# When a group's input rows are loaded in the query stage

## What is computed

```python
h = modulate(layernorm(x), shift_msa, scale_msa)
qkv = h @ W_qkv + b_qkv                  # 576 -> 3 * 576
o = softmax(q * scale @ k.T) @ v         # 16 heads of 36
x = x + gate_msa * (o @ W_proj + b_proj)
x = x + gate_mlp * (gelu(modulate(layernorm(x)) @ W_fc1 + b_fc1) @ W_fc2 + b_fc2)
# rotation: U, _ = qr(P); R = expm(A(cond)); x + ((x @ U) @ R - x @ U) @ U.T
```

## Time and profile before

| | us |
|---|---|
| median of 3 runs | 3202.49 |
| lowest and highest | 3201.93 and 3209.22 |
| the profiled execution, its time | 3204.2 |
| its span | 3202.5 |
| TensorE (PE) busy in it | 2868.2 (90%) |
| VectorE (DVE) busy | 1638.2 (51%) |
| ScalarE (ACT) busy | 1457.6 (46%) |
| GpSimd (POOL) busy | 1438.2 (45%) |

### The profile page before, as it was taken

The page is one execution under the profiler, slowest core; times in us unless marked ns, Lnnn a source line. Parts: engine busy times, 40 slices in busy tenths (PEclk is TensorE's granted clock), DMA queues, the critical chain, the costliest instruction groups (busy, mean ns, idle before and its releaser), DMA issues. The chain is left out here.

```text
span 3202.5 us, 49786 instructions
## 1 busy us (share of the span) xinstructions
PE 2868.2 (90%) x16066; PEld 2278.3 (71%) x16066; DVE 1638.2 (51%) x2847; ACT 1457.6 (46%) x1863; POOL 1438.2 (45%) x1065
## 2 busy tenths in 40 slices
PE   6859999979999999999999677869999999999976
PEld 3147878856666666666566466759999999999965
DVE  3446666558888888888888546501111111111125
ACT  2112222238888898888888635521111111111112
POOL 1233332128888888888888735422222222222200
PEclk9869999979999999999999878879999999999988
DMA  5466665653334333333333267693211211211153
GB/s 172 139 217 219 226 221 206 230 142 78 89 80 91 77 90 81 86 90 79 91 78 90 75 179 217 201 303 113 71 36 36 71 36 36 71 36 36 51 152 140
DMA packets 340330, 378.72 MB, mean 118 GB/s; under 512 B 167008, under 2 KB 230120, under 8 KB 340188
## 3 DMA queue, kind: packets, MB, share of 16 engines
q1 hardware_dynamic: 328494, 354.69, 37.2%
q0 software_dynamic: 4224, 9.44, 1.6%
q10 hardware_dynamic: 7474, 12.68, 1.3%
HBM read 226.82 MB, written 158.93 MB: 120 GB/s over the span
## 5 line engine op out<-in xcount | busy, mean ns | idle before, releaser
L811 POOL TENSOR_TENSOR a_pl<-a_pf,a_ph 128x1024 fp32r<-128x1024 f32 x384 | 913.5, 2399 | 46.7 <-ACT a_pf L899 46.2
L834 DVE TENSOR_REDUCE a_mx<-a_psum_s 128x1 f32<-128x1024 f32 x496 | 606.4, 1223 | 177.3 <-PE a_psum_s L910 169.2
L897 ACT ACTIVATE a_ph<-a_psum_t 128x1024 fp32r<-128x1024 f32 x512 | 526.2, 1028 | 143.5 <-PE a_psum_t L942 125.4
L1545 PE MATMUL m_psum_h<-m_ht,m_w 128*128 128x256 f32 x4032 | 534.5, 284 | 30.9 <-DMA m_w<-w_s 21.9
L1497 POOL TENSOR_TENSOR m_al<-m_af,m_ah 128x256 fp32r<-128x256 f32 x288 | 213.1, 740 | 763.2 <-DVE m_ah L1506 763.2
L1545 PEld LDWEIGHTS m_psum_h<-m_ht,m_w 128*128 128x128 f32 x4032 | 508.9, 190 | 34.2 <-issue 34.2
L1506 DVE CAST m_ah<-m_af 128x256 fp32r<-128x256 f32 x288 | 84.6, 294 | 849.0 <-ACT m_af L1483 849.0
L1483 ACT ACTIVATE m_af<-m_psum_h,m_bias 128x256 f32<-128x256 f32 x288 | 137.0, 476 | 815.1 <-PE m_psum_h L1545 815.1
L1559 PE MATMUL m_psum_y<-m_w,m_ah 128*128 128x288 f32 x2304 | 504.9, 296 | 1.4 <-DVE m_y L1523 1.2
L961 PE MATMUL a_psum_o<-a_ph,a_vs 128*100 128x512 f32 x1024 | 405.7, 396 | 3.7 <-POOL a_pl L811 3.6
L962 PE MATMUL a_psum_o<-a_pl,a_vs 128*100 128x512 f32 x1024 | 404.2, 395 | 0.0
(11 more groups left out here) (222 smaller groups left out, 3097.6 us busy)
## 6 DMA issues: line engine op xcount, KB each, us to landing
a_qs<-q_s SPq DMA_DIRECT2D x192, 144.0 KB
a_ks<-k_s SPq DMA_DIRECT2D x192, 144.0 KB
w_s<-q_ws SPq DMA_DIRECT2D x64, 324.0 KB, 3.5
h_s<-p_ht SPq DMA_DIRECT2D x40, 512.0 KB, 5.2
m_ht<-h_s SPq DMA_DIRECT2D x16, 1280.0 KB, 8.4
v_s<-q_vo SPq DMA_DIRECT2D x64, 288.0 KB, 2.3
a_vs<-v_s SPq DMA_DIRECT2D x128, 144.0 KB, 4.5
q_s<-q_qko SPq DMA_DIRECT2D x32, 512.0 KB, 2.9
```

What stands on the lines that cost most here:

```text
L811: pool.tensor_tensor(pl[:, s % RING], pf[:, s % RING], raw(ph[:, s % RING]), ALU.subtract).then_inc(lo_pool, 1)
L834: dve.tensor_reduce(mx[:, u % 2, t:t + 1], p_s[:], AX.X, ALU.max).then_inc(s_free, 1)
L897: act.activation(ph[:, s % RING], p_t[:, s % 2], ACT.Exp, scale=SCALE)
L1545: m = pe.matmul(p_h[:, f % RING, 0:GM], w1[:, k, f * P:(f + 1) * P], ht[:, q, a], start=(i == 0), stop=(i == len(PASSES) - 1))
```

## The change

SP's program for the query stage alone is changed. Up to now the load of the rows of group g + 2 stood at the head of group g, ahead of m = 0. Now the load of group g + 3 stands in group g ahead of the store of m = 7 (`QKM - 2`), behind the issues of m = 6. It waits for `xn_ready` and `lo_ready` of group g + 1, whose buffer it fills. The load of group 2 keeps its place at the head of group 0. The loop runs over b = 0 and 1, and groups 4 to 7 are written out, so that the loads end with group 7's.

```diff
-                def body(b, half, last):
+                sp.wait_ge(xn_ready, 1)
+                sp.wait_ge(lo_ready, NK)
+                load(1, 0)
+
+                def load_ahead(b, half):
+
                     g = 2 * b + half
-                    if not last:
-                        wait_alone(sp, xn_ready, g + 1, passed)
-                        sp.wait_ge(lo_ready, NK * (g + 1))
-                        load(b + 1, half)
+                    wait_alone(sp, xn_ready, g + 2, passed)
+                    sp.wait_ge(lo_ready, NK * (g + 2))
+                    load(b + 1 + half, 1 - half)
+
+                def body(b, half, more):
+                    g = 2 * b + half
+                    last = isinstance(b, int) and b == B - 1
                     for m in range(QKM):
+                        if more and m == QKM - 2:
+                            load_ahead(b, half)
 
                         sp.wait_ge(qk_lo[m % QR], START + (QKM // QR) * g + m // QR + 1)
...
-                groups(nc.sync, body)
+                with sp.Fori(0, B - 2) as b:
+                    body(b, 0, True)
+                    body(b, 1, True)
+                for g in range(2 * (B - 2), 2 * B):
+                    body(g // 2, g % 2, g + 3 < 2 * B)
```

## The result

The changed kernel took 3185.48 us (median of 4 runs, 3183.0 to 3187.11), the kernel before beside it 3205.85 (median of 4, 3201.93 to 3212.2). The ratio is 0.994, with a 95% interval of 0.9927 to 0.9952. Forecast were 3186.6 us, a ratio of 0.995.

A forecast was written before the change was run, and what follows sets the result against it. TensorE was taken to bound the query stage; bringing groups 1 to 5 to group 2's 54.77 us gains 15.9 us (5.2 waits, 1.3 transposes' waits, some 9 half clock), giving 3186.6 us, range 3181 to 3194.

The forecast's parts named there:

- The bound and the place: Query stage: TensorE bounds it, busy 52.72 of 54.77 us in group 2; only its stalls and reduced clock can be won.
- The moved load: SP's queue: xt issued 24 us ahead of its group's start lands in time, so VectorE's five waits go to nothing.
- The wait in two parts, 2.0 us of VectorE's own and the lag: TensorE's chain-step wait in groups 1 to 5: about 2.0 us stays, the lag (1.43 us in group 1) goes.
- Where the lag comes from: VectorE in groups 1 to 5: late xt, waited for 22.9 us in five waits, makes all its later work late.
- The clock: TensorE in groups 1, 3, 4, 5: half clock follows the longer waits, not group 2's 2.05 us; some 9 us gained.
- The first rival: TensorE's clock falls behind the remaining waits too: 3193.5 us with three of five groups, up to 3201.6; chance 0.13.
- The added waits and the issues: SP ahead of m = 7's store: waits on xn_ready and lo_ready and about 1.1 us of issues cost nothing.
- the tight place: Weight block for m = 8, just ahead of xt in SP's queue: cost taken as 0, at most 4 us in five groups.
- The second rival: Block for m = 8 shares the queue's engines with xt and lands late: slower, 3217 us; chance 0.04.
- The rest of the time: Attention, projection and MLP behind the stage start earlier by the same 15.9 us and do nothing else.

The follow-up runs named there:

- e1: Changed kernel with the early load moved back from m = 7 to just ahead of the stores of t = 3: 3190.7 us, ratio 0.9952 to the kernel before.
- e5: Changed kernel with VectorE's chain step of m = 5 ahead of that tile's two evictions: 3181.76 us, ratio 0.9936 to the kernel before.
- e10: Changed kernel with VectorE's m = 5 chain step ahead of its evictions and, at m = 4, the statistics' end ahead of line 411's work: 3177.5 us, ratio 0.9918.
- e9: Kernel before, load of xt at the group's head, with three buffers for weight blocks instead of two: 3199.35 us, ratio 0.9984.
- e11: The changed kernel itself measured once more: 3189.92 us, ratio 0.9959 to the kernel before.
- e7: Changed kernel with two more row statistics on VectorE at m = 4 of groups 0 to 5: 3189.81 us, ratio 0.9958 to the kernel before.
- e2: Changed kernel with an added 1152 KB store of xt to spare DRAM at the head of groups 0 to 5: 3186.32 us, ratio 0.9944 to the kernel before.

## Why the prediction was right, step by step

*The bound and the place.* Right: all that changed by the edit lies in groups 1 to 5 of one stage, and TensorE is busy without a gap in group 6 before and after.

*The moved load.* Right. It was put at 24 us ahead of T and lands unnoticed. e1 shows how much of that is reserve: 0.6 us ahead of T is enough. What the prediction did not ask is why xt came earlier in group 2 than in group 1, though it was issued later after T: there it landed in 5.8 us instead of 8.4.

*The wait in two parts, 2.0 us of VectorE's own and the lag.* Right, and the step that carries the forecast. The waits that stay are 1.90 to 1.98 us against the 2.05 that was taken from group 2; the 0.15 us a group between 54.77 and the 54.62 measured are the 0.75 us by which the stage's gain of 16.65 exceeds the 15.9. e5 and e10 confirm what the 2 us consist of: take the two evictions and GpSimd's shadow out of the way and 0.3 us is left.

*Where the lag comes from.* Named as the wait for xt alone; e9 makes it some two thirds of it in groups 1, 3 and 5. The rest came from the blocks of weights that stand behind xt in SP's queue. The sum did not suffer, since the change takes both away.

*The clock.* Half right. The gain was split into 6.5 us of waits and some 9 of half clock. Measured over groups 1 to 5, TensorE's idle time fell by 7.1 us (16.7 to 9.6) and its busy time by 9.6, and in the profiled execution nothing fell behind the short waits. But that a wait of 2 us leaves the clock up, which the prediction took from group 2 alone, is not true as a rule: 7 of 34 such waits brought it down, and one of the changed kernel's own groups is among them (e11). The first rival is thus real and was priced about right for one group (six of the seven falls cost about 1.5 us, one about 3), only rarer than the three groups in five that its example assumed. That none of the five fell in the profiled execution is in part luck: at 7 of 34 it happens in about one execution of three, by an estimate that takes the groups as independent. Together with the kernel before, whose long waits fell each time but cost now 1.5 and now 3 us, it is one source of the spread of the runs; how much of that spread it makes was not measured, since only profiled executions show the clock.

*The added waits and the issues.* Right at nothing: SP issues xt at 461.18, 0.1 us after its issue before ends, so it does not wait there. Block m = 8, the tight place, is not waited for in any of the changed kernel's groups: in groups 1 to 4 it lands at T + 33.1 to T + 34.2, ahead of xt (T + 37.0 to T + 37.4) and of ScalarE, which wants it at T + 36.7. What stands behind xt did land later, the store of m = 7 at T + 38.5 instead of T + 36.7 in group 2, and no engine waited for it. The second rival (slower through the queue) did not occur.

*The rest of the time.* The profiled span fell by 17.5 us, 0.9 us more than the stage's groups gave; the ratios of 0.994 and 0.9959 in two comparisons hold the forecast 0.995 between them.

## What to carry to other kernels

Split a wait of the bounding engine into the part that its releaser's own work makes and the part that comes from the releaser's lateness, by comparing like groups of the same trace; an earlier transfer removes only the second. Look for the group that already has the input in time: its duration is the forecast for the others. Behind a stall count the clock as well as the idle time, since here more than half of the gain was the same matmuls at full instead of half clock.

## What was not expected of the hardware

- The granted clock fell behind 7 of 34 waits of 1.87 to 2.30 us, 4 of 5 of 2.41 to 2.48, and all 10 of 2.81 to 3.79, at a price of about 1.5 or about 3 us. Something beside the wait's length decides; that it is its moment is not shown. The Trainium skill's page "TensorE: Matmul & The Clock Gate", section "What's actually happening", has the gate keep its own schedule; unequal outcomes of equal waits agree with that.
- A VectorE operation on 128 × 4 elements took 1.08 us beside a GpSimd operation (changed kernel), 0.17 us away from it (e10), and 0.36 us when it began near that operation's end (e7).
- 1152 KB more in the queue at the head of each group (e2: a store of 4.6 to 5.8 us) cost groups 2 to 5 nothing (54.58 to 54.69 us), with the DMA engines at a share of 0.73, 0.73, 0.74 and 0.67. Group 1 took 56.17 us, by a fall of the clock that e11 has in the same group without the store.
